# A rotation, three transformer layers and a mixture of experts on one core: layer 0 rearranged over the engines

## The chip, the cores and the metric

The kernel runs on one core of a Trainium2 chip. A core has TensorE (PE), VectorE (DVE), ScalarE (ACT), GpSimd (POOL) and SyncE (SP), which here issues the DMAs. Each works through its own list of instructions in order and waits on semaphores. Matmul results land in PSUM, eight banks of 512 fp32 columns; the other operands lie in SBUF. The metric is the device time of one execution in microseconds; three runs of the kernel before gave 2080.91 to 2091.76 us, median 2091.69.

## The reference

The input is `x` of 4 x 512 x 288 and one condition vector of 288 numbers per batch. Layer 0 comes first:

```python
U, _ = jnp.linalg.qr(P)                      # P is 288 x 64
R = expm(A)                                  # A skew, 64 x 64 per batch, its entries silu(cond) @ W.T + b
z = einsum('btn,nd->btd', x, U)
x = x + einsum('btd,nd->btn', einsum('btd,bde->bte', z, R) - z, U)
```

Three transformer layers follow. Each forms `mod = silu(c) @ w_ada + b_ada`, split in six vectors of 288 (shift, scale and gate of the attention and of the MLP), then a layernorm with shift and scale, attention with 16 heads of 18, its gated projection, a second layernorm with shift and scale, and a gated MLP of width 1152. The last layer's MLP is a mixture of four experts with the best two of each token. All is fp32.

## The kernel before

**Layer 0.** QR is done without forming the long columns. The Gram matrix of P (64 x 64) stands beside a unit matrix in `GI` (64 x 128), and the top 64 rows of P in `T`. For each of 64 columns j, PE spreads row j of `GI` over all partitions (`spread_gram`, L1416: a product with a repeated column of the unit matrix), and DVE eliminates with it (`reduce_gram`, L878 to L885). PE spreads row j of `T` as well (`spread_top`, L1423), and DVE forms sign, root and divisor and updates `T` (`reduce_top`, L895 to L910). POOL takes the square root (L733, a `pow`). `reduce_top` runs one column behind `reduce_gram`. What comes out is `RT`, which turns P into the orthonormal columns.

Between two columns PE does background work, each piece in a slot of the table `BACKGROUND` (the number is the column ahead of whose `spread_top` it stands):
- `skew`: the entries of the skew matrix, column by column, 378 instructions with up to 63 stationary columns and 4 moving ones (L1453); `turn`: its transpose (L1460). DVE adds bias and scales.
- `exp`: expm by a series of degree 6 and 14 squarings, so 19 rounds. A round is two halves of 8 products of 64 x 64 (L1476 with the matrix, L1477 with the unit matrix, which adds it); ACT copies a round's bank back (L1234).
- `x`, `y`: transposes of x (L1432) and y = P' x for each batch (L1441).
- `ada`: the modulation vectors of all three layers, three times ten pieces. The four vectors wanted along the partitions are products with 4 moving columns (L1497), the two gates products of 288 columns (L1502).

Then come the product of `RT` and expm into `Mid` (L1525, L1528), and for each batch `YM` = `Mid` y (L1535), x += `YM` PT (L1542, DVE L976). A barrier of all engines ends this phase.

**The opening.** Work is laid out in ticks: `opening()` gives the first 27 ticks (`PTICKS`), and `agenda` makes each engine's list of it. For batch 0: statistics (`stats1`, `mean1` on DVE), root and shift on POOL, normalised rows on ACT, three transposed pieces (`ln1`, L1653), five q and k pieces (`qk`) and four v pieces (`v`, both L1550), the trip of q and k through HBM into `QK` (`place`), and the first 32 score tiles (`warm`, L1572), of which DVE takes the row maxima (L996).

**Attention and MLP** follow tick by tick; the first instruction of attention proper is the first key score (L1587).

## Time and profile before

| | |
|---|---|
| runs | 2080.91 to 2091.76 us, median 2091.69 |
| the profiled execution's own time | 2106.0 us |
| its span, first to last instruction | 2104.2 us |
| PE busy, matmul | 1904.2 us (90%) |
| DVE, ACT, POOL busy | 1233.4, 924.5, 547.0 us |
| mean granted TensorE clock | 0.911 of 2.4 GHz |
| first key score (L1587) | 347.0 us |

A profile is of one execution. Busy time of PE is the time in which some matmul is in flight, and not a measure of how full the array is: an instruction of 4 moving columns counts as one of 512. PE lists each fp32 product as two instructions. The granted clock of a stretch (PEclk) reads 1.00 at 2.4 GHz and 0.50 at 1.2 GHz.

### The profile page before, as it was taken

The numbers are of one execution on the slowest core, as the hardware profiler recorded it, in microseconds if no ns is written. First come the engines' busy times: TensorE is split into PE (matmuls) and PEld (weight loads), VectorE is DVE, ScalarE is ACT, GpSimd is POOL, SyncE is SP. The second block draws the span as 40 slices with busy tenths as digits, with TensorE's granted clock in tenths as the row PEclk, the third lists the DMA queues.
The fourth block names the chain that finished last, engine by engine and source line by source line (L and its number), as shares of the span: only waits on it lengthen the run. The fifth ranks groups of instructions, "written<-read, shape, count | busy, mean of one in ns | idle before, by whom it ended". The sixth has DMA issues, their size and how long they took to land.

```text
span 2104.2 us, 29869 instructions
## 1 busy us (share of the span) xinstructions
PE 1904.2 (90%) x10842; PEld 1298.8 (62%) x10842; DVE 1233.4 (59%) x2748; ACT 924.5 (44%) x1582; POOL 547.0 (26%) x541
## 2 busy tenths in 40 slices
PE   7899858999989878999978998999989889999998
PEld 6687534444438766444435876444438778888997
DVE  6755526777735456777742655777734655546554
ACT  0200023766664434777654533767573432222221
POOL 1111131222245533333233533222141220101000
PEclk9965567999989988999987999999989999999999
DMA  7000013333210021232220021332300010001000
GB/s 236 1 1 1 8 46 93 95 101 90 93 34 10 1 80 58 86 97 79 79 73 20 4 80 50 96 106 87 104 26 35 20 31 16 26 23 34 1 23 23
DMA packets 68985, 114.08 MB, mean 54 GB/s; under 512 B 14586, under 2 KB 29498, under 8 KB 68840
## 3 DMA queue, kind: packets, MB, share of 16 engines
q1 hardware_dynamic: 68840, 112.18, 17.6%
q8 instruction: 87, 1.43, 0.3%
q14 instruction: 58, 0.48, 0.1%
HBM read 80.95 MB, written 30.70 MB: 53 GB/s over the span
## 4 chain that ended last, share of the span: by engine, by line
PE 72%; ACT 10%; DVE 9%; issue 4%; DMA 2%; POOL 2%; SPq 1%; ACTq 0%; DVEq 0%; POOLq 0%
PE ps L1550 23%; PE ps L1632 13%; PE ps L1601 8%; PE ps L1587 7%; PE ps L1678 5%; PE ps L1572 4%; ACT Pr L1373 3%; PE ps L1497 2%; PE ps L1653 2%; PE ps L1453 2%; ACT xn L1272 1%; DVE negmax L996 1%; ACT HQ L1348 1%; PE ps L1476 1%; PE ps L1477 1%
## 5 line engine op out<-in xcount | busy, mean ns | idle before, releaser
L996 DVE TENSOR_REDUCE negmax<-ps 128x1 f32<-128x512 f32 x768 | 490.1, 683 | 185.1 <-PE ps L1572 179.4
L1373 ACT ACTIVATE Pr<-ps 128x512 f32<-128x512 f32 x768 | 406.8, 601 | 155.1 <-PE ps L1587 153.6
L1384 ACT ACTIVATE g<-ps,b1col 128x512 f32<-128x512 f32 x216 | 148.5, 687 | 451.9 <-PE ps L1550 439.1
L1180 DVE CAST G<-g 128x512 fp32r<-128x512 f32 x216 | 125.9, 583 | 323.8 <-ACT g L1384 322.9
L1587 PE MATMUL ps<-QK 55*128 55x512 f32 x768 | 249.3, 515 | 53.9 <-ACT Pr L1373 51.6
L1632 PE MATMUL ps<-W2a,G 128*128 128x288 f32 x1728 | 269.7, 307 | 2.0 <-DVE G L1182 2.0
L1632 PEld LDWEIGHTS ps<-W2a,G 128*128 128x128 f32 x1728 | 251.8, 196 | 14.8 <-DVE G L1182 4.2
L1587 PEld LDWEIGHTS ps<-QK 55*128 55x128 f32 x768 | 98.4, 194 | 242.6 <-ACT Pr L1373 142.8
L1572 PE MATMUL ps<-QK 54*128 54x512 f32 x768 | 202.8, 437 | 29.2 <-DVE negmax L996 17.1
L1601 PE MATMUL ps<-Pr,V 128*32 128x512 f32 x1536 | 222.0, 652 | 0.0
L1182 DVE TENSOR_TENSOR G<-g,G 128x512 fp32r<-128x512 f32 x216 | 167.0, 773 | 7.4
L1550 PE MATMUL ps<-HQ,W1a 128*128 128x512 f32 (+1 forms) x504 | 137.4, 414 | 12.8 <-ACT g L1384 11.4
L1572 PEld LDWEIGHTS ps<-QK 54*128 54x128 f32 x768 | 95.7, 194 | 59.3 <-DVE negmax L996 38.1
L1632 PEld LDWEIGHTS ps<-W2b,G 128*128 128x128 f32 x864 | 123.1, 188 | 8.5 <-DVE G L1182 2.4
L1632 PE MATMUL ps<-W2b,G 128*128 128x288 f32 x864 | 127.1, 296 | 1.1 <-DVE G L1182 1.1
L787 POOL TENSOR_TENSOR stage<-act,stage 126x512 fp32r<-126x512 f32 (+1 forms) x60 | 77.2, 1287 | 185.7 <-ACT stage L1365 137.8
L1550 PEld LDWEIGHTS ps<-HQ,W1a 128*128 128x128 f32 (+1 forms) x504 | 94.5, 197 | 37.2 <-ACT g L1384 17.1
L1550 PEld LDWEIGHTS ps<-WQ,HQ 128*128 128x128 f32 (+1 forms) x560 | 80.5, 196 | 55.1 <-issue 22.9
L1550 PE MATMUL ps<-WQ,HQ 128*128 128x288 f32 (+1 forms) x560 | 98.6, 317 | 14.2 <-ACT HMq L1348 4.8
L1678 PE MATMUL ps<-WP,oT 128*128 128x288 f32 x384 | 110.6, 433 | 0.1
L787 POOL TENSOR_TENSOR HQ<-act,HQ 128x512 fp32r<-128x512 f32 (+1 forms) x54 | 69.6, 1289 | 140.3 <-ACT HQ L1348 139.9
L792 POOL TENSOR_TENSOR oTok<-oTok,rsum 128x512 f32<-128x512 f32 x48 | 50.3, 1049 | 208.7 <-DVE rsum L1108 207.7
(205 smaller groups left out, 2652.7 us busy)
## 6 DMA issues: line engine op xcount, KB each, us to landing
QK<-heads_t SPq DMA_DIRECT2D x192, 144.0 KB
heads_t<-stage SPq DMA_DIRECT2D x96, 252.0 KB
QK<-heads_t SPq DMA_DIRECT2D x192, 72.0 KB
raw<-in_w SPq DMA_DIRECT2D x18, 432.0 KB
raw<-in_w SPq DMA_DIRECT2D x12, 576.0 KB
WA<-in_ada_w SPq DMA_DIRECT2D x3, 1728.0 KB, 15.5
heads_t<-stage SPq DMA_DIRECT2D x24, 144.0 KB
QK<-W1a SPq DMA_DIRECT2D x192, 2.0 KB, 2.4
```

What stands on the lines that cost most here:

```text
L787: pool.tensor_tensor(lo, act32[rows, h % 2, :], hi.bitcast(F32), ALU.subtract).then_inc(low_done, 1)
L996: dve.tensor_reduce(negmax[:, m % 2, t, h:h + 1], ps[:, a_bank(s, i), :], AX, ALU.max, negate=True).then_inc(a_free, 1)
L1180: dve.tensor_copy(G[:, n % 3, 0, :], g32[:, n % 2, :]).then_inc(g_hi, 1)
L1182: dve.tensor_tensor(G[:, n % 3, 1, :], g32[:, n % 2, :], G[:, n % 3, 0, :].bitcast(F32), ALU.subtract).then_inc(g_lo, 1)
L1373: act.activation(Pr[:, t % 2, 2 * half + pair, :], ps[:, (16 * s + u) % 3, :], ACT.Exp, scale=SCALE).then_inc(b_free, 1)
L1384: act.activation(g32[:, n % 2, :], ps[:, 4, :], ACT.Gelu if l == 1 else ACT.Gelu_apprx_tanh, bias=b1col[:, e, s % FT:s % FT + 1]).then_inc ...
L1550: ins = mm(o, lhs(w, h, rows[w]), rhs(w, h, rows[w]), start=p == 0, stop=p == 6)
L1572: mm(ps[:, a_bank(s, i), :], QK[r:r + QROW, g, 0, pair, 128 * t:128 * t + 128], QK[r:r + QROW, g, 1, pair, :], start=True, stop=True).then ...
L1587: mm(ps[:, k % 3, :], QK[r:r + QROW + 1, g, 1, pair, 128 * t:128 * t + 128], QK[r:r + QROW + 1, g, 0, pair, :], start=True, stop=True).the ...
L1601: ins = mm(ps[32 * i:32 * i + 32, 6, :], V[:, s // 4 % 2, t, c:c + 32], Pr[:, t % 2, i, :], start=t == 0, stop=t == TT - 1)
L1632: ins = mm(ps[:, t, 0:C], G[:, n % 3, x, 128 * t:128 * t + 128], W2[e % 2][:, w, ft, :], start=ft == 0 and p == 0, stop=ft == FT - 1 and p ...
L1678: ins = mm(bank[:, 0:C], oT[:, (STEPS * l + 4 * i + g) % 5, 128 * k:128 * k + 128], WP[:, g, :], start=g == 0, stop=g == 3)
```

## The change

It touches layer 0, the modulation vectors and the opening:
- **Columns.** `GI` is updated in the 64 columns that are still live, `T` and its helper in those right of j. PE spreads row j twice, into one bank for DVE (65 columns) and another for ACT. ACT copies it with a factor 4 (`gram_copy`), POOL raises its diagonal entry to 0.5 and -0.5 in one instruction (`root_pair`), ACT scales the row with the second (`gram_scale`). `reduce_top` runs two columns behind.
- **Skew.** The entries of all four batches come as one row each, four times three products of 512 columns, the bias as one more row of the weights. They go to HBM and come back as 64 x 64 matrices; DVE masks them, ACT scales.
- **Expm.** A round is 8 products. The unit matrix is added ahead of it by POOL (`add_unit`, 64 x 256, two per round), and a round stands in every second column.
- **Modulation.** Each vector is a row of 4 x 288 from three products (`row_product`), bias and the 1 of the scale included in the weights. Those wanted along the partitions are turned by five small products (`turn_columns`) and copied by ACT. The six of the first transformer layer stand in the columns, the other twelve in the opening.
- **Opening.** `Mid` y and the update of x become items of the opening, batch 0 first; it has 34 ticks, and the first scores use five banks in turn. The weight splits of ACT and POOL stand in the columns (`high`, `split`), the rows of ones for `QK` are placed early.

```diff
+    for b, (t, u) in enumerate(((0, 1), (2, 3), (6, 7), (9, 10))):
+        out += [(t, "ym", 0, b, 0), (u, "l0", 0, b, 0)]
+    out += [(1, "stats1", 0, 0, t) for t in range(TT)] + [(1, "mean1", 0, 0, 0)]
+    out += [(t, "ln1", 0, 0, c) for c, t in enumerate((5, 7, 9))]
...
+    rows = [(2, 1, 0), (3, 1, 1), (4, 1, 2), (6, 1, 3), (8, 1, 4), (10, 1, 5),
+            (12, 2, 0), (16, 2, 1), (18, 2, 2), (20, 2, 3), (22, 2, 4), (24, 2, 5)]
+    for t, l, v in rows:
+        out += [(t, "arow", l, v, 0)] + ([(t + 1, "acol", l, v, 0)] if v not in (2, 5) else [])
+    out += [(t, "qk", 0, 0, j) for j, t in enumerate((11, 13, 17, 20, 23))]
...
+            def add_unit(r):
+                unit = (ident[0:D, 0:D] if r < DEGREE - 1 else ident2[:, :]).unsqueeze(1).broadcast_to([D, B, D])
+                for x in range(2):
+                    pool.wait_ge(exp_ev, 2 * r + x + 1)
+                    pool.tensor_tensor(EM[:, r % 2, x], EX[:, r % 2, x], unit, ALU.add).then_inc(exp_add, 1)
+                    pool.wait_ge(exp_add, 2 * r + x + 1)
+            def root_pair(j):
+                pool.wait_ge(g_copied, j + 1)
+                pool.tensor_tensor(roots[:, j, :], RG[:, j % 2, j:j + 1].broadcast_to([D, 2]), halves[:, :], ALU.pow).then_inc(root_ready, 1)
...
+            for j in range(D):
+                root_pair(j)
+                for slot, kind, *args in BACKGROUND:
+                    if kind == "split" and slot == j:
+                        low_weights(*args)
+                    if kind == "turn" and slot + 2 == j:
+                        add_unit(0)
+                    if kind == "exp" and slot == j and args[0] < ROUNDS - 1:
+                        add_unit(args[0] + 1)
...
             def reduce_gram(j):
-                k, r, m = j % 2, small[:, j % 2, 0:1], small[:, j % 2, 2:3]
-                row = ps[0:D, k, 0:2 * D]
+                row, m, r = ps[0:D, 0, 0:2 * D], small[:, 0:1], small[:, 5:6]
+                live = slice(j + 1, j + 1 + D)
                 dve.wait_ge(bc_g, j + 1)
                 dve.reciprocal(r, row[:, j:j + 1]).then_inc(dve_done, 1)
                 dve.wait_ge(dve_done, step())
                 dve.scalar_tensor_tensor(out=m, in0=GI[:, j:j + 1], scalar=r, in1=below[:, j:j + 1],
                                          op0=ALU.mult, op1=ALU.mult).then_inc(dve_done, 1)
                 dve.wait_ge(dve_done, step())
-                dve.scalar_tensor_tensor(out=GI[:, :], in0=row, scalar=m, in1=GI[:, :],
+                dve.wait_ge(bc_r, j + 1)
+                dve.scalar_tensor_tensor(out=GI[:, live], in0=row[:, live], scalar=m, in1=GI[:, live],
                                          op0=ALU.mult, op1=ALU.add).then_inc(gi_upd, 1)
-                dve.tensor_copy(RG[:, k, :], row[:, 0:D]).then_inc(n2_ready, 1)
             def reduce_top(j):
-                k = j % 2
-                n2, root = RG[:, k, j:j + 1], small[:, k, 1:2]
-                sg, den, rd, m, nb = small[:, k, 3:4], small[:, k, 4:5], small[:, k, 5:6], small[:, k, 6:7], NB[:, j:j + 1]
-                row = ps[0:D, 2 + k, 0:D]
-                alpha = row[:, j:j + 1]
+                row, sh = ps[0:D, 1, 0:D], SH[:, j:j + 1]
+                den, m, rd = small[:, 1:2], small[:, 2:3], small[:, 6:7]
+                alpha, live = row[:, j:j + 1], slice(j + 1, D)
                 dve.wait_ge(bc_t, j + 1)
-                dve.tensor_scalar(sg, alpha, 0.0, 2.0, ALU.is_ge, ALU.mult).then_inc(dve_done, 1)
+                dve.tensor_scalar(sh, alpha, 0.0, 0.5, ALU.is_ge, ALU.subtract).then_inc(dve_done, 1)
                 dve.wait_ge(dve_done, step())
-                dve.wait_ge(n2_root, j + 1)
-                dve.wait_ge(n2_ready, j + 1)
-                dve.tensor_scalar(nb, sg, -1.0, root, ALU.add, ALU.mult).then_inc(dve_done, 1)
-                dve.wait_ge(dve_done, step())
-                dve.tensor_scalar(den, alpha, nb, n2, ALU.mult, ALU.add).then_inc(dve_done, 1)
+                if j == D - 1:
+                    return
+                dve.wait_ge(g_scaled, j + 1)
+                dve.tensor_scalar(den, sh, roots[:, j, 0:1], alpha, ALU.mult, ALU.add).then_inc(dve_done, 1)
                 dve.wait_ge(dve_done, step())
                 dve.reciprocal(rd, den).then_inc(dve_done, 1)
+                ready = step()
+                dve.scalar_tensor_tensor(out=W[:, live], in0=RG2[:, j % 2, live], scalar=sh, in1=row[:, live],
+                                         op0=ALU.mult, op1=ALU.add).then_inc(dve_done, 1)
+                step()
+                dve.wait_ge(dve_done, ready)
+                dve.scalar_tensor_tensor(out=m, in0=T[:, j:j + 1], scalar=rd, in1=below[:, j:j + 1],
+                                         op0=ALU.mult, op1=ALU.mult).then_inc(dve_done, 1)
                 dve.wait_ge(dve_done, step())
-                dve.scalar_tensor_tensor(out=m, in0=T[:, j:j + 1], scalar=rd, in1=below[:, j:j + 1],
-                                         op0=ALU.mult, op1=ALU.mult)
-                dve.scalar_tensor_tensor(out=RG[:, k, :], in0=row, scalar=nb, in1=RG[:, k, :],
-                                         op0=ALU.mult, op1=ALU.add).then_inc(dve_done, 1)
-                dve.wait_ge(dve_done, step())
-                dve.scalar_tensor_tensor(out=T[:, :], in0=RG[:, k, :], scalar=m, in1=T[:, :],
+                dve.scalar_tensor_tensor(out=T[:, live], in0=W[:, live], scalar=m, in1=T[:, live],
                                          op0=ALU.mult, op1=ALU.add).then_inc(t_upd, 1)
...
+                act.activation(RG[:, j % 2, j:D], ps[0:D, 2 + j % 2, j:D], ACT.Copy, scale=4.0).then_inc(g_copied, 1)
...
+                act.activation(RG2[:, j % 2, j + 1:D], RG[:, j % 2, j + 1:D], ACT.Copy, scale=roots[:, j, 1:2]).then_inc(g_scaled, 1)
...
             def spread_gram(j):
                 pe.wait_ge(gi_upd, j + 1)
+                mm(ps[0:D, 0, j:j + D + 1], ident[:, j:j + 1].broadcast_to([128, D]), GIz[:, j:j + D + 1],
+                   start=True, stop=True).then_inc(bc_g, 1)
                 if j >= 2:
-                    pe.wait_ge(n2_ready, j - 1)
-                k = j % 2
-                mm(ps[0:D, k, 0:2 * D], ident[:, j:j + 1].broadcast_to([128, D]), GIz[:, :],
-                   start=True, stop=True).then_inc(bc_g, 1)
+                    pe.wait_ge(g_copied, j - 1)
+                mm(ps[0:D, 2 + j % 2, j:D], ident[:, j:j + 1].broadcast_to([128, D]), GIz[:, j:D],
+                   start=True, stop=True).then_inc(bc_r, 1)
             def spread_top(j):
                 if j > 0:
                     pe.wait_ge(t_upd, j)
-                k = j % 2
-                mm(ps[0:D, 2 + k, 0:D], ident[:, j:j + 1].broadcast_to([128, D]), Tz[:, :],
+                mm(ps[0:D, 1, j:D], ident[:, j:j + 1].broadcast_to([128, D]), Tz[:, j:D],
                    start=True, stop=True).then_inc(bc_t, 1)
...
+                for c, rows in enumerate((128, 128, 33)):
+                    ins = mm(ps[0:B, 6 + n % 2, :], csil[0:rows, c, :], Wsk[0:rows, c, N * n:N * n + N], start=c == 0, stop=c == 2)
+                ins.then_inc(skew_mm, 1)
...
+            def exp_round(r):
                 if r == 0:
...
+                for x in range(2):
+                    pe.wait_ge(exp_ev, 2 * r + 2)
+                    pe.wait_ge(exp_add, 2 * r + x + 1)
+                    for b in range(B):
+                        left = BB[:, 1 - x, b, :] if r < DEGREE - 1 else EX[:, r % 2, 1 - x, b, :]
+                        ins = mm(ps[0:D, 6 + x, D * b:D * b + D], left, EM[:, r % 2, x, b, :], start=True, stop=True)
+                    ins.then_inc(exp_mm, 1)
...
+            def row_product(l, v, bank):
+                n = AROW["arow", l, v, 0]
+                if v == 0:
                     pe.wait_ge(ada_in[l], 32)
                     pe.wait_ge(silu_done, 1)
+                if n > 0:
+                    pe.wait_ge(arow_ev, n)
+                    pe.wait_ge(acol_ev, sum(m < n for key, m in AROW.items() if key in ACOL))
+                if n == 0:
                     pe.wait_ge(y_ev, B)
...
+                for c, rows in enumerate((128, 128, 34)):
+                    ins = mm(ps[0:B, bank, 0:C], csil[0:rows, c, :], WA[l][0:rows, c, C * v:C * v + C], start=c == 0, stop=c == 2)
+                ins.then_inc(arow_mm, 1)
...
+            def turn_columns(l, v, bank):
+                n = AROW["arow", l, v, 0]
+                pe.wait_ge(arow_ev, n + 1)
+                for c in range(3):
+                    for r in range(1 if c < 2 else 3):
+                        rows = 128 if c < 2 else 32
+                        ins = mm(ps[32 * r:32 * r + rows, bank, C + B * c:C + B * c + B],
+                                 arow[:, n % 2, 128 * c:128 * c + rows], ident[0:B, 0:B], start=True, stop=True)
+                ins.then_inc(acol_mm, 1)
...
 BACKGROUND = sorted(
+    [(4 + 3 * n, "skew", n) for n in range(4)] + [(20, "turn")] + [(23 + 2 * r, "exp", r) for r in range(ROUNDS)] +
+    [(t, "x", n // 3, n % 3) for n, t in enumerate((15, 16, 17, 19, 21, 22, 26, 28, 30, 34, 36, 38))] +
+    [(t, "y", b) for b, t in enumerate((18, 24, 32, 40))] +
+    [(t, "high", n) for n, t in enumerate((28, 32, 46))] + [(t, "split", n) for n, t in enumerate((29, 33, 47))] +
+    [(50, "bias", 0)] +
+    [(t, "arow", 0, v, 5) for v, t in enumerate((42, 46, 50, 52, 56, 60))] +
+    [(t, "acol", 0, v, 5) for v, t in ((0, 44), (1, 48), (3, 54), (4, 58))], key=lambda x: x[0])
```

On DVE, one column as it repeats (before; `GI`, `T` as above, `RG` the copied row, `NB` sign and root):

```order
L878 RECIPROCAL small<-ps 64x1
L880 SCALAR_TENSOR_TENSOR small<-GI,small,below 64x1
L883 SCALAR_TENSOR_TENSOR GI<-ps,small,GI 64x128
L885 COPY RG<-ps 64x64
L895 TENSOR_SCALAR small<-ps 64x1
L899 TENSOR_SCALAR NB<-small 64x1
L901 TENSOR_SCALAR small<-ps,NB,RG 64x1
L903 RECIPROCAL small<-small 64x1
L905 SCALAR_TENSOR_TENSOR small<-T,small,below 64x1
L907 SCALAR_TENSOR_TENSOR RG<-ps,NB,RG 64x64
L910 SCALAR_TENSOR_TENSOR T<-RG,small,T 64x64
```

and now (`SH` is the sign as 0.5 or -0.5, `RG_126` the row scaled by ACT, `W` the helper):

```order
L966 RECIPROCAL small<-ps 64x1
L968 SCALAR_TENSOR_TENSOR small<-GI,small,below 64x1
L972 SCALAR_TENSOR_TENSOR GI<-ps,small,GI 64x64
L981 TENSOR_SCALAR SH<-ps 64x1
L986 TENSOR_SCALAR small<-SH,roots,ps 64x1
L988 RECIPROCAL small<-small 64x1
L990 SCALAR_TENSOR_TENSOR W<-RG_126,SH,ps 64x62
L994 SCALAR_TENSOR_TENSOR small<-T,small,below 64x1
L997 SCALAR_TENSOR_TENSOR T<-W,small,T 64x62
```

Eleven instructions become nine, and the widths shrink with the column.

On PE, a column with expm and y work before (`EF`, `BB` are the matrices of expm):

```order
L1423 MATMUL ps<-T,ident 64x64
L1416 MATMUL ps<-GI,ident 64x128
L1476 MATMUL ps<-EF,BB 64x64
L1477 MATMUL ps<-ident,BB 64x64
L1476 MATMUL ps<-EF,BB 64x64
L1477 MATMUL ps<-ident,BB 64x64
L1476 MATMUL ps<-EF,BB 64x64
L1477 MATMUL ps<-ident,BB 64x64
L1476 MATMUL ps<-EF,BB 64x64
L1477 MATMUL ps<-ident,BB 64x64
L1441 MATMUL ps<-XT,Psb 64x512 x3
L1423 MATMUL ps<-T,ident 64x64
```

and two columns with an expm round and a transpose now (`EM` is the matrix with the unit added):

```order
L1525 MATMUL ps<-GI,ident 64x65
L1530 MATMUL ps<-GI,ident 64x29
L1545 MATMUL ps<-ident,X 128x128 x4
L1536 MATMUL ps<-T,ident 64x31
L1525 MATMUL ps<-GI,ident 64x65
L1530 MATMUL ps<-GI,ident 64x28
L1583 MATMUL ps<-EM,EX 64x64 x8
L1536 MATMUL ps<-T,ident 64x30
```

One round took sixteen products, eight in a column, and takes eight in one column of two.

On PE, the end of layer 0 and the opening before (`YT`, `YM`, `PT`, `HQ_58` the layernormed x):

```order
L1535 MATMUL ps<-YT,Mid 64x512 x2
L1542 MATMUL ps<-PT,YM 128x288 x4
L1535 MATMUL ps<-YT,Mid 64x512
L1542 MATMUL ps<-PT,YM 128x288 x4
L1535 MATMUL ps<-YT,Mid 64x512
L1542 MATMUL ps<-PT,YM 128x288 x8
L1653 MATMUL ps<-ident,xn 128x128 x8
L1653 MATMUL ps<-ident,xn 96x128 x4
L1550 MATMUL ps<-HQ_58,WQ 126x512 x14
L1550 MATMUL ps<-WQ,HQ_58 128x288 x7
L1550 MATMUL ps<-HQ_58,WQ 126x512 x7
L1550 MATMUL ps<-WQ,HQ_58 128x288 x7
```

and now, with `WA_103` the modulation weights of the second layer:

```order
L1744 MATMUL ps<-YT,Mid 64x512
L1752 MATMUL ps<-PT,YM 128x288 x4
L1744 MATMUL ps<-YT,Mid 64x512
L1598 MATMUL ps<-WA_103,csil 4x288 x3
L1752 MATMUL ps<-PT,YM 128x288 x4
L1607 MATMUL ps<-ident,arow 128x4 x2
L1607 MATMUL ps<-ident,arow 32x4 x3
L1598 MATMUL ps<-WA_103,csil 4x288 x3
L1607 MATMUL ps<-ident,arow 128x4 x2
L1607 MATMUL ps<-ident,arow 32x4 x3
L1598 MATMUL ps<-WA_103,csil 4x288 x3
L1769 MATMUL ps<-ident,xn 128x128 x4
```

The four updates of x stood together; now the first stands alone, and row products and turned columns stand between the others and the layernorm.

## Rows read from the trace of the kernel before

**Rows 1.** Windows, all engines: start:end, length, busy us (x instructions), PEclk, DMA share, GB/s.

```profile
62.00:120.00 58.00, 50.26 (x418) 35.40 (x418) 42.83 (x218) 13.52 (x23) 10.84 (x20) 0.94 0.01 2
120.00:256.00 136.00, 124.07 (x856) 103.68 (x854) 74.38 (x363) 6.50 (x11) 20.24 (x32) 0.57 0.01 2
256.00:281.00 25.00, 15.80 (x50) 8.13 (x50) 10.64 (x28) 7.43 (x13) 7.01 (x8) 0.77 0.03 8
281.00:347.00 66.00, 43.77 (x124) 25.43 (x124) 21.48 (x38) 17.18 (x29) 15.67 (x15) 0.58 0.30 92
347.00:2104.20 1757.20, 1622.24 (x8951) 1085.79 (x8950) 1046.61 (x1933) 875.91 (x1502) 484.07 (x440) 0.95 0.18 54
```

**Rows 2.** Chain that ended last, 8 to 256 us, share by line.

```profile
by line: PE ps L1497 18.6%; PE ps L1453 12.9%; PE ps L1476 9.0%; PE ps L1477 8.9%; PE ps L1416 8.2%; PE ps L1423 6.6%; PE ps L1502 6.0%; PE ps L1441 4.4%; issue 3.4%; DVE small L901 2.5%; DVE GI L883 2.2%; DVE T L910 2.1%; DVE small L905 2.
```

**Rows 3.** Instruction groups of PE, 8 to 256 us: busy us, mean ns.

```profile
L1497 PE MATMUL ps<-csil,WA 128*32 128x4 f32 (+1 forms) x360 | 52.3, 257 | 4.8 <-DVE grow L948 4.8
```

**Rows 4.** Timeline of DVE, one column: start us, duration us, instruction.

```profile
97.40 0.28 DVE L910 SCALAR_TENSOR_TENSOR T<-RG,small,T 64x64 f32<-64x64 f32 x1
97.60 0.15 DVE L878 RECIPROCAL small<-ps 64x1 f32<-64x1 f32 x1
97.79 0.21 DVE L880 SCALAR_TENSOR_TENSOR small<-GI,small,below 64x1 f32<-64x1 f32 x1
98.04 0.34 DVE L883 SCALAR_TENSOR_TENSOR GI<-ps,small,GI 64x128 f32<-64x128 f32 x1
...
98.44 0.14 DVE L895 TENSOR_SCALAR small<-ps 64x1 f32<-64x1 f32 x1
98.61 0.21 DVE L899 TENSOR_SCALAR NB<-small 64x1 f32<-64x1 f32 x1
98.86 0.27 DVE L901 TENSOR_SCALAR small<-ps,NB,RG 64x1 f32<-64x1 f32 x1
99.16 0.15 DVE L903 RECIPROCAL small<-small 64x1 f32<-64x1 f32 x1
99.35 0.21 DVE L905 SCALAR_TENSOR_TENSOR small<-T,small,below 64x1 f32<-64x1 f32 x1
99.49 0.27 DVE L907 SCALAR_TENSOR_TENSOR RG<-ps,NB,RG 64x64 f32<-64x64 f32 x1
99.79 0.28 DVE L910 SCALAR_TENSOR_TENSOR T<-RG,small,T 64x64 f32<-64x64 f32 x1
```

**Rows 5.** Timeline of PE and DVE, the two hand-offs of a column.

```profile
95.67 0.33 PE L1423 MATMUL ps<-T,ident 128*64 128x64 f32 x2
...
96.04 0.15 DVE L895 TENSOR_SCALAR small<-ps 64x1 f32<-64x1 f32 x1 [1.91 <-PE ps L1423]
...
97.73 0.33 PE L1423 MATMUL ps<-T,ident 128*64 128x64 f32 x2 [0.92 <-DVE T L910]
...
98.43 0.69 PE L1416 MATMUL ps<-GI,ident 128*64 128x128 f32 x2 [0.38 <-DVE GI L883]
```

**Rows 6.** Timeline of PE, three products of 512 and of 288 columns.

```profile
92.86 2.88 PE L1441 MATMUL ps<-XT,Psb 128*64 128x512 f32 x6
...
200.42 3.13 PE L1502 MATMUL ps<-WA,csil 128*4 128x288 f32 x6
```

**Rows 7.** Timeline of POOL and DVE, 247 to 252 us.

```profile
247.98 4.08 POOL L738 TENSOR_TENSOR WQ<-raw,WQ 128x864 fp32r<-128x864 f32 x2
...
250.22 1.92 DVE L910 SCALAR_TENSOR_TENSOR T<-RG,small,T 64x64 f32<-64x64 f32 x1
```

**Rows 8.** Timeline of POOL and DVE, 1640 to 1643 us.

```profile
1640.76 1.45 POOL L751 TENSOR_TENSOR rstd<-var,neghalf 128x4 f32<-128x4 f32 x1
...
1641.69 0.69 DVE L1182 TENSOR_TENSOR G<-g,G 128x512 fp32r<-128x512 f32 x1
```

**Rows 9.** Timeline of PE, first `ln1` product and first key scores.

```profile
281.17 1.09 PE L1653 MATMUL ps<-ident,xn 128*128 128x128 f32 x4 [8.43 <-ACT xn L1275]
...
347.00 1.21 PE L1587 MATMUL ps<-QK 55*128 55x512 f32 x2
```

563 lines of the change are left out of this document (293 added, 270 removed).

## The prediction

> **What bounds the kernel now.** I read the windows first, cut where the work changes. The QR and expm phase ends at 256 us, the opening (the layer 0 update, the first layernorm, q, k, v of batch 0 and the first scores) takes from there to 347 us, and the remaining 1757.2 us run at a granted clock of 0.95 [rows 1, 9]. The change leaves the instructions behind 347 us in their order, so I look for its whole effect ahead of that point. In the chain of waits of 8 to 256 us nearly every named share is PE's [rows 2]: the modulation products (L1497) 18.6%, the skew products (L1453) 12.9%, the expm products (L1476 and L1477) 17.9%, against 6.8% of the three DVE lines that it still lists in full or in part. In the last 136 us of it PE is busy 124 at a granted clock of 0.57 [rows 1], so most of that work ran at the lower level, 1.2 GHz.
>
> The second view is the timeline of one column that no background work of PE holds up. DVE needs 2.39 us for it (97.40 to 99.79, from one T to the next) [rows 4]. 64 columns of that are 153 us, while 248 pass between 8 and 256. The other 95 us are PE work that stands between two columns and is not covered. Both parts are touched by the change.
>
> **The column.** From 11 DVE instructions it goes to 9: the copy of the row goes to ACT, the scaling by the root to ACT and POOL, and GI is updated in 64 columns, not 128. I put it together from start-to-start distances of rows 4: reciprocal to m 0.19, m to GI 0.25, GI (64 wide, like T to reciprocal) 0.20, sign to den 0.17, den to its reciprocal 0.30, that to W 0.14 (as L905 to L907, no wait between), W to m 0.20, m to T 0.25, T to the next reciprocal 0.20. That is 1.90, and about 1.85 as W and T grow narrower. PE has to keep up in that time. T to the start of its product takes 0.33 and from there to the sign 0.37 [rows 4, 5], 0.70 in all, while DVE has 0.84 of other work in between, so it doesn't wait. Sum: column 0 starts near 5.8 us (an estimate: two memsets stand ahead of it on DVE instead of eight, two loads fewer are waited for), first two columns 2.7, 62 columns of 1.85 are 115, the end 2: 125.5 us.
>
> **PE work between the columns.** After GI PE starts 0.39 later [rows 4, 5], spreads two rows of 65 and on average 32 columns, and is wanted again by T one column on. By these distances 0.9 us are free at the higher clock and 0.7 at the lower: background beyond some 0.8 us per column shows. Prices: three products of 512 columns take 2.9 us at 2.4 GHz, three of 288 take 3.1 at 1.2 GHz [rows 6]. So three of 512 are 2.6 to 5.1 without the tail, three of 288 are 1.5 to 3.0, eight of 64 are 0.9 to 1.8.
> - Skew, 378 tiny matmul instructions now, becomes 4 rows of three 512-column products. I take 3.5 each, 2.7 uncovered: 11 us.
> - Four y products of the same size: 11 us. Twelve transposes nearly fit: 2 us.
> - Expm: 19 rounds of 8 products instead of 16, one round every second column. I take 1.3 each, 0.5 uncovered: 9 us.
> - Row products of the first transformer layer, six at 2.2: 8 us; their four turned columns: 2 us. The turn of the skew matrix, where PE waits for DVE and DVE for PE: 2 us. Its trip through HBM lies between columns 13 and 20, over 12 us, and costs nothing; without that cover it would be some microseconds, once.
> - POOL. It now adds the unit, 64x256 twice a round. One 128x864 subtraction takes 2.04 [rows 7], so 256 columns are about 0.6. Beside those two subtractions L910, which reads two tiles in SBUF, took 1.92 us instead of 0.28 [rows 4, 7] and ended with the second of them. Three DVE instructions of a new column have two such inputs (both m and T). 38 additions of 0.6, hitting at any phase, delay by 0.2 each on average where DVE isn't waiting anyhow: 7 us. The three weight splits that move from behind the columns into them delay by most of their 2.04: 5 us.
>
> Uncovered: 57 us. Bounds: all at 2.4 GHz and POOL's additions in DVE's own waits, 22; all at 1.2 GHz and each addition fully waited for, 106. The columns then end at 182.5 us (147 to 231), where they end at 256 now: 73 us earlier. ACT and POOL have 2.4 columns, over 4 us, for the hand-over of a row (copy, root, scale), which I cost at nothing.
>
> **The rule that speaks against it.** The Trainium skill, page "SBUF — State Buffer", section "SBUF: two separate sides", says of the port pair that VectorE and GpSimd share that the one that starts first has it for its whole instruction and the other is blocked entirely. The T of rows 7 agrees with it. The root (`pow`) does not: while L751 ran from 1640.76 to 1642.21, an L1182 with two inputs in SBUF started at 1641.69 and took its usual 0.69 [rows 8]. So I count the 64 roots at nothing. What the root would cost if it did hold the port is a rival below.
>
> **The opening.** It takes 91 us now, with PE busy 15.8 of 25 and 43.8 of 66 us, so 31 idle, at clocks of 0.77 and 0.58 [rows 1]. Into it come 12 row products (1.5 to 3.0) and 8 turned columns. For one of these I take 10 matmul instructions at the 257 ns of L1497 [rows 3], which overlap by half, hence 0.8 to 1.6. Together that is 24 to 49 us of PE work, in a stretch that becomes denser, so nearer to the lower end: 34. They stand between the pieces of the q, k, v chain, whose waits are PE's idle time; I let 22 be filled. The update of batch 0 ahead of the others lets the statistics start some 9 us sooner, but PE has to pass the other three updates before the first q product in any case; I count 4. 91 + 34 - 22 - 4 = 99 us. Bounds: 87 (all of it in idle time) to 140 (nothing is hidden, low clock).
>
> **Sum.** First scores of attention at 182.5 + 99 = 281.5 instead of 347: 65.5 us less. The profiled execution took 2106.0 us, so 2040.5 by its own measure. It lies 14 us above the median of 2091.69 shown, so the forecast for a median is 2026 us, 3.1% faster.
>
> **Rivals.**
> - *High clock and full cover.* PE's dense streams of 288 and 512 columns keep the clock up, and the row products vanish in idle time. Columns end at 155, opening 91: 246, so 101 us less, 1991. For: in 62 to 120 us the clock read 0.94 with such streams [rows 1]. Against: between the streams the new columns ask still less of PE. Chance 0.17.
> - *The root holds the port*, or the hand-over over ACT and POOL comes late. By the distances of rows 4 and 5 the root starts about 1.4 us after GI and ends 0.6 or 0.7 later, and the m of the next GI stands at 1.58: it would wait 0.5 in each of 62 columns, 31 us: 2057. This is what the skill's rule makes of it; rows 8 speak against. Chance 0.15.
> - *Slower: the opening becomes a chain on one bank.* All 12 row products and 8 columns go through PSUM bank 4, each waits for ACT's copy of the last, and whatever stands behind on PE waits with it. At 1.2 GHz that is 49 us of work and 20 hand-overs; at 1.5 us each with no idle time used, 79 more: 170. With the columns at 213 (the rival above) that is 383, 36 us later than now: 2128. It decides once columns and opening together exceed 347. Against it: 31 us of idle PE, and other banks for everything else. Chance 0.03.
> - *The shorter rounds don't shorten anything*, because each waits for ACT and POOL, and no more than 0.5% is gained. A ring of PE, two copies and two additions of 0.6 needs about 4 us, two columns 3.7. Chance 0.02.
>
> **Numbers.** Forecast 0.63, its own range 2010 to 2044. With the rivals the range is 1993 to 2062. A change under 0.5% (10 us) could not be told from none. Faster 0.95, same 0.02, slower 0.03.
>
> **What would show it.** Right: the last column near 180 us, columns without background near 1.85 us, first key scores near 280, the rest within 1757 us and a few. POOL's additions beside a stretched m or T, and none beside a root. Wrong: every column over 2.3 us with a stretched m (the port), PE idle in columns while DVE waits for the scaled row (the hand-over), an opening well over 110 us with PE waiting for ACT's copies of rows (the bank), or a change behind the first scores, which no step here allows for.

## The result: 1.0% faster where 3.1% was forecast

The changed kernel takes 2069.6 us in the median of 5 runs (2061.37 to 2071.78), the kernel before 2087.11 beside it (2080.91 to 2091.76): ratio 0.9903, 95% interval 0.9875 to 0.9932. The same kernel, run once more for the experiments, gives 2064.93 and 0.9893 (0.9872 to 0.9915). The direction is right. The gain is some 20 us, a third of the 65.5 that I summed up, and the time lies above the range of 1993 to 2062.

Windows of the changed kernel, cut where its work changes (columns as in [rows 1]):

```profile
62.00:120.00 58.00, 49.38 (x304) 33.90 (x302) 39.08 (x182) 22.20 (x74) 30.79 (x40) 0.59 0.03 7
120.00:195.00 75.00, 67.38 (x408) 44.78 (x409) 44.00 (x234) 21.41 (x90) 34.01 (x47) 0.52 0.00 1
195.00:318.00 123.00, 98.21 (x325) 45.27 (x326) 31.87 (x66) 28.12 (x66) 19.36 (x21) 0.62 0.14 42
318.00:2059.60 1741.60, 1599.77 (x8951) 1072.07 (x8949) 1046.69 (x1933) 878.63 (x1504) 485.35 (x441) 0.96 0.18 55
```

The QR and expm phase ends at 195 us instead of 256, 61 earlier. The opening takes 123 us instead of 91, and gives 32 of them back. The granted clock is 0.59, 0.52 and 0.62 in the three stretches: in 62 to 120 us, where [rows 1] had 0.94, it is low as well.

A column that no background work holds up, by DVE's timeline of the changed kernel. It answers to [rows 4], and POOL's root beside it is the last row:

```profile
114.42 0.24 DVE L997 SCALAR_TENSOR_TENSOR T<-W,small,T 64x29 f32<-64x29 f32 x1
114.59 0.15 DVE L966 RECIPROCAL small<-ps 64x1 f32<-64x1 f32 x1
114.78 0.21 DVE L968 SCALAR_TENSOR_TENSOR small<-GI,small,below 64x1 f32<-64x1 f32 x1
115.02 0.28 DVE L972 SCALAR_TENSOR_TENSOR GI<-ps,small,GI 64x64 f32<-64x64 f32 x1
115.29 0.15 DVE L981 TENSOR_SCALAR SH<-ps 64x1 f32<-64x1 f32 x1
...
116.24 0.24 DVE L997 SCALAR_TENSOR_TENSOR T<-W,small,T 64x28 f32<-64x28 f32 x1
```
```profile
114.44 0.70 POOL L815 TENSOR_TENSOR roots<-RG,halves 64x2 f32<-64x2 f32 x1
```

T to T is 1.82 us (forecast 1.85). The root ran from 114.44 to 115.14, and a T and an m (L968) with two inputs in SBUF took their usual 0.24 and 0.21 beside it: no wait for the port. Beside a weight split it is otherwise:

```profile
93.63 2.05 DVE L997 SCALAR_TENSOR_TENSOR T<-W,small,T 64x35 f32<-64x35 f32 x1
```
```profile
93.63 2.00 POOL L822 TENSOR_TENSOR WQ<-raw,WQ 128x864 fp32r<-128x864 f32 x1
```

What one piece of background costs PE, from the chain of waits (start, duration): two skew rows, a y product, an expm round.

```profile
13.99 4.61 PE ps L1565 x6
...
23.31 5.30 PE ps L1565 x6
...
58.09 4.76 PE ps L1554 x6
...
73.19 1.90 PE ps L1583 x16
```

[Rows 6] has 2.88 for three products of 512 columns at the higher level; these are nearer to the lower one, as the granted clock of 0.59 and 0.52 says. I had taken 3.5, 3.5 and 1.3.

The opening, first on PE and then on ACT. L1598 is a row product, L1769 a turn of xn, L1637 a q or v product, L1663 the query scores:

```profile
215.52 3.13 PE L1598 MATMUL ps<-WA,csil 128*4 128x288 f32 x6 [0.44 <-ACT ada L1340]
219.14 1.22 PE L1607 MATMUL ps<-ident,arow 4*128 4x4 f32 x10 [0.49 <-ACT arow L1333]
220.79 3.13 PE L1598 MATMUL ps<-WA,csil 128*4 128x288 f32 x6 [0.44 <-ACT ada L1340]
226.94 1.12 PE L1769 MATMUL ps<-ident,xn 128*128 128x128 f32 x4 [3.02 <-ACT xn L1376]
...
261.65 1.20 PE L1637 MATMUL ps<-WQ,HQ 128*128 128x288 f32 x7 [1.24 <-ACT stage L1478]
275.23 1.22 PE L1663 MATMUL ps<-QK 54*128 54x512 f32 x4 [12.38 <-DMA QK<-heads_t]
```
```profile
223.96 0.40 ACT L1333 ACTIVATE arow<-ps 4x288 f32<-4x288 f32 x1 [3.31 <-PE ps L1598]
224.27 2.17 ACT L1373 ACTIVATE xn<-X,shift,rstd 128x288 f32<-128x288 f32 x4
```

PE has 12.38 us of idle time in one piece, waiting for the DMA of the heads, and no row product stands there. Seven stand ahead of it and five behind it, and ACT scales xn only after the third row copy.

### The profile page after: what moved, and what is told of

Read it like the earlier page. It is cut to its first block, busy times and chain, and to the rows that moved or that the text cites. A ratio compares the mean times of both kernels' runs of the same rounds, so it can differ in the third digit from the quotient of the medians.

```text
span 2059.6 us, 28854 instructions
## 1 busy us (share of the span) xinstructions
PE 1862.0 (90%) x10144; PEld 1215.4 (59%) x10144; DVE 1192.9 (58%) x2584; ACT 964.4 (47%) x1778; POOL 584.9 (28%) x585
## 4 chain that ended last, share of the span: by engine, by line
PE 72%; ACT 10%; DVE 9%; issue 4%; DMA 2%; POOL 1%; SPq 1%; ACTq 0%; DVEq 0%; POOLq 0%
PE ps L1637 23%; PE ps L1726 13%; PE ps L1695 8%; PE ps L1681 7%; PE ps L1794 5%; PE ps L1663 4%; ACT Pr L1486 3%; PE ps L1598 2%; PE ps L1769 2%; ACT xn L1373 2%; PE ps L1583 1%; DVE negmax L1050 1%; DVE X L1068 1%; ACT HQ L1461 1%; DMA heads_t<-stage 1%
## 5 line engine op out<-in xcount | busy, mean ns | idle before, releaser
L1726 PE MATMUL ps<-W2a,G 128*128 128x288 f32 x1728 | 263.8, 303 | 7.2 <-DVE G L1241 5.7
L1726 PEld LDWEIGHTS ps<-W2a,G 128*128 128x128 f32 x1728 | 245.8, 192 | 20.5 <-DVE G L1241 10.4
L1663 PE MATMUL ps<-QK 54*128 54x512 f32 x768 | 198.9, 433 | 33.4 <-DVE negmax L1050 14.9
L1695 PE MATMUL ps<-Pr,V 128*32 128x512 f32 x1536 | 217.2, 639 | 0.0
L1637 PE MATMUL ps<-HQ,W1a 128*128 128x512 f32 (+1 forms) x504 | 134.5, 407 | 12.8 <-ACT g L1497 11.4
L1663 PEld LDWEIGHTS ps<-QK 54*128 54x128 f32 x768 | 93.1, 192 | 61.1 <-DVE negmax L1050 34.3
L1637 PEld LDWEIGHTS ps<-HQ,W1a 128*128 128x128 f32 (+1 forms) x504 | 93.2, 194 | 36.0 <-ACT g L1497 16.4
L1637 PEld LDWEIGHTS ps<-WQ,HQ 128*128 128x128 f32 (+1 forms) x560 | 79.4, 193 | 51.9 <-issue 24.2
L1637 PE MATMUL ps<-WQ,HQ 128*128 128x288 f32 (+1 forms) x560 | 97.1, 314 | 12.5 <-ACT HMq L1461 4.8
```

The costliest lines, as they stand in the source:

```text
L1637: ins = mm(o, lhs(w, h, rows[w]), rhs(w, h, rows[w]), start=p == 0, stop=p == 6)
L1663: mm(ps[:, row_bank(l, s, i), :], QK[r:r + QROW, g, 0, pair, 128 * t:128 * t + 128], QK[r:r + QROW, g, 1, pair, :], start=True, stop=True) ...
L1695: ins = mm(ps[32 * i:32 * i + 32, 6, :], V[:, s // 4 % 2, t, c:c + 32], Pr[:, t % 2, i, :], start=t == 0, stop=t == TT - 1)
L1726: ins = mm(ps[:, t, 0:C], G[:, n % 3, x, 128 * t:128 * t + 128], W2[e % 2][:, w, ft, :], start=ft == 0 and p == 0, stop=ft == FT - 1 and p ...
```

## Experiments

Each kernel was timed against the kernel before in five rounds on the same chip; ratios are to that. "Columns end" is the first product with RT (194.8 in the changed kernel's first profile), "opening" the time from there to the first key scores.

**1. The changed kernel again.** No edit.

> The changed kernel as it is, once more. In the two profiles so far the first key scores come at 318.1 us instead of 347.0 (28.9 earlier), and what lies behind them is 15.7 us shorter, 44.7 in all, while the medians differ by 17.5. Theory A: the stretch behind the first scores varies from execution to execution, and the true gain is about 20 us: the ratio to the kernel before comes out at 0.990, the first key scores of a new profile at 318 within 2 us, and the rest behind them at more than 1745. Rival B: the later layers really are shorter: ratio near 0.980, the rest again at 1741.5.

2064.93 us, ratio 0.9893. Columns end at 193.6, first key scores at 320.4, the rest is 1746.2. Theory A holds, though the first scores lie just outside its 318 within 2 us.

**2. The kernel before again.** No edit.

> The kernel before, once more, for a profile that is not 19 us above its median. Its first key scores come at 347.0 in the first profile, the changed kernel's at 318.1 and 320.4, so 27 to 29 are won ahead of them, but the medians differ by 20 to 22. Theory A (part of it is given back behind the first scores): in this profile the first scores come again at 347 and what lies behind them takes 1740 or less, against 1741.5 and 1746.2 in the changed kernel. Rival B (the rest is alike and the profile of before was only an outlier in its opening): first scores at 340, rest 1745.

Ratio 0.9984 (0.9961 to 1.0008). Its windows:

```profile
62.00:120.00 58.00, 50.35 (x410) 35.23 (x411) 42.44 (x216) 13.55 (x23) 10.87 (x20) 0.94 0.01 2
120.00:247.00 127.00, 114.51 (x865) 95.64 (x863) 74.78 (x365) 6.50 (x11) 20.28 (x32) 0.63 0.01 3
247.00:338.00 91.00, 59.63 (x174) 33.60 (x175) 32.12 (x66) 24.58 (x41) 22.70 (x23) 0.63 0.23 69
338.00:2088.00 1750.00, 1610.83 (x8951) 1077.51 (x8950) 1045.93 (x1933) 875.32 (x1502) 484.50 (x440) 0.96 0.18 54
```

Here the columns end at 247, not 256 [rows 1], at a clock of 0.63 instead of 0.57 behind 120 us. The first scores come at 337.8. Rival B is nearer: the first profile of before was 9.2 us late ahead of the first scores and 7 behind them (1757.2 against 1750). Nothing is given back behind the first scores: 1750 and 1746 in these two executions. Taken from this pair, the change wins 17.5 us ahead of them and 4 behind.

**3. Wide rows.**

```
-ps[0:B, 6 + n % 2, :], csil[0:rows, c, :]   # csil [128, 3, 4]
+ps[:, 6 + n % 2, :], csil[0:rows, c, :]     # csil [128, 3, 128], the 4 columns 32 times
```

> The skew rows and all 18 row products are made with csil repeated 32 times, so that they fill 128 rows of PSUM instead of 4; number of instructions and streamed columns are the same. Theory 1 (PE's clock is the mis-sized term): before the change the clock stayed at 1.00 until 80 us with wide products, after it fell to 0.53 at 20 us when the skew rows (4 rows of output) began. With wide ones the clock in 20 to 60 us is 0.9 or more, a skew row takes 2.7 us instead of 5.3, a row product 1.6 to 2.3 instead of 3.1; columns end 8 to 15 us earlier than 194.8, and the first key scores come 15 to 30 us earlier than 318.1: ratio to before 0.975 to 0.985. Rival 2 (the number of waits and small pieces between the columns sets the clock): granted clock and the 4.8 and 3.1 us stay as they are, time the same as the changed kernel within 3 us.

2068.56 us, ratio 0.9915 (0.9895 to 0.9935). Columns end at 193.3, first scores at 321.2. The four skew rows took 4.23, 4.86, 5.23 and 5.79 us. The clock of 20 to 60 us reads 0.66, but the columns end where they did: those with a y product are 2.4 us shorter in all than in experiment 1, those with a row product 2.5 longer, since a wide row product takes 3.55 us where the narrow one takes 3.13. The time is rival 2's.

**4. Wide rows and wide expm products.** As 3, with EX, EM and BB on 128 partitions (64 of zeros) and `left` two blocks wide where it can be.

> As the kernel with the wide rows, and the expm products get 128 contracted rows (64 of them zeros, as they had before the change) and mostly 128 rows of output instead of 64 by 64. Theory 1: an expm round falls from 1.93 to 1.1 us, so that the clock in 80 to 190 us rises from 0.5 to 0.6 up to 0.8 or more, columns end at 175 us or before, first key scores below 295, ratio to before 0.96 to 0.975. Rival 2: the rounds stay at 1.9 us and the time at that of the kernel with wide rows alone.

2101.86 us, ratio 1.0078 (1.0053 to 1.0102): slower than the kernel before. Columns end at 227.9. PE's timeline of it, a skew row and an expm round, and the window around the skew row:

```profile
36.36 5.79 PE L1572 MATMUL ps<-Wsk,csil 128*128 128x512 f32 x6
...
118.34 3.85 PE L1593 MATMUL ps<-EM,EX 128*128 128x64 f32 x16
```
```profile
36.00:42.00 6.00, 6.00 (x10) 1.94 (x9) 1.36 (x8) 0.00 (x0) 0.00 (x0) 1.00 0.21 69
```

The eight products with 128 rows and (mostly) 128 outputs take 3.85 us instead of 1.97 at the same clock, and 2.17 at the higher one. The granted clock rose little for it: 0.67 instead of 0.59 from 60 to 120 us, and 0.53 in both from 120 to 180. So the round of 64 by 64 is cheap at 1.2 GHz already, and widening it doubles its price for almost no clock. Theory 1 was half wrong: the price at the lower clock is the mis-sized term, but not one that these edits give back. The window shows why I had misread it. It says 1.00 while three products of 512 columns take 5.79 us, more than a y product takes in the stretches of 0.5 to 0.6 (4.76). The trace's clock records begin at 51.4 us here and at 17.8 us in the changed kernel; ahead of the first record a window reads 1.00 whatever the speed. The "fall at 20 us" on which this expectation rests was the first record.

**5. Rows in attention.** All 12 row products and 8 turned columns leave the opening and go through bank 7 into the attention of layer 0.

```
-for t, l, v in rows: out += [(t, "arow", l, v, 0)] ...      # opening, bank 4
+if l == 0 and b < 2: ... out += [(t, "arow", b + 1, v, 0)]  # attention window, bank 7
```

> The 12 row products and 8 turned columns of the second and third transformer layer leave the opening and go through bank 7 into the attention of layer 0, batches 0 and 1. Theory 3 (they stand in order in the opening, with ACT's scaling of xn behind them): the opening falls from 123.4 us to 95 or less (12 times 3.1 and 8 times 1.2 are 47 us of PE work, and 15 us in which xn waited for ACT), first key scores at 290 or earlier; attention of layer 0, with PE busy 95%, takes 12 times 1.6 and 8 times 0.6, some 24 us, more than its 275, so that the time is within 10 us of the changed kernel. Rival 4 (the opening is bound by its own chain of q, k, v and the DMA of the heads, the row products only fill its waits): opening 115 us or more, and the time 15 to 25 us worse than the changed kernel's.

2049.4 us, ratio 0.9824 (0.9802 to 0.9847), 0.7% better than the changed kernel. Opening 91.0 us instead of 126.8 in experiment 1; attention of layer 0 291.1 instead of 272.6. Theory 3 holds for the opening and the attention; the time is 15.5 us below the changed kernel's, where it had said within 10. First query and first key scores on PE:

```profile
248.74 1.22 PE L1676 MATMUL ps<-QK 54*128 54x512 f32 x4 [12.15 <-DMA QK<-heads_t]
...
283.86 0.63 PE L1694 MATMUL ps<-QK 55*128 55x512 f32 x2
```

From the end of the columns to the first query scores it is 55.9 us, with the rows 83.8: 27.9 more. Seven row products and five turned columns stood there: 7 x 3.13 and 5 x 1.2 are 27.9 (27.4 by their durations in experiment 1). They cost their work one for one, and the wait of 12 us stayed beside it.

**6. Rows in the gap.** As 5, but rows 0, 1 and 2 of the second layer stand in the opening behind the first v product.

> As the kernel with the rows in attention, but three of the row products and two of the turned columns come back into the opening, behind the first v product, where PE waits 12.15 us for the DMA of the heads. Theory 3 (it is the place in PE's order that costs, not the work): at 1.2 GHz they are 3 times 3.1 and 2 times 1.2 with five hand-overs of 0.5, 14 us, of which 12 are covered; first key scores at 284 to 287, attention of layer 0 some 6 us shorter, time 3 to 5 us better than the kernel with all rows in attention. Rival 4 (opening bound elsewhere, pieces of PE there cost in full): first key scores at 298, time 6 us or more worse.

2061.06 us, ratio 0.9859 (0.9826 to 0.9892). First query scores at 263.7, 14.5 us after those of 5 by their distance from the columns' end: the rival's number, but not its reason. SP's queue shows it:

```profile
232.66 1.61 SPq L692 DMA_DIRECT2D heads_t<-stage  x2
251.36 0.26 SPq L680 DMA_DIRECT2D gate_rows<-arow  x1
251.66 1.52 SPq L692 DMA_DIRECT2D heads_t<-stage  x2
257.16 0.32 SPq L709 DMA_DIRECT2D QK<-heads_t  x1
```

The DMA of the gate row waits on SP for the third row copy, and the second store of heads, ready near 237, waits behind it until 251.66.

**7. The splits behind the columns, too.** As 6, with `(28, 32, 46)` and `(29, 33, 47)` of BACKGROUND taken out and "split" items at ticks 3, 3 and 6 of the opening. ACT's halves of the splits, the bias and one load move with POOL's.

> As the kernel with rows in the gap, and POOL's three weight splits go out of the columns into the opening. Theory 5 (a split holds up the m or T of the column beside it: 93.63 2.05 T, 108.25 1.94 den, 148.81 2.06 T): the columns end 5 to 6 us earlier and the time is 4 to 6 us better. Rival 6 (PE is the bound in those columns too, so a late T is covered by its background): columns end within 1.5 us of before, time the same within 2 us, or worse, because the splits now hold up the layer 0 update.

2051.29 us, ratio 0.981 (0.9777 to 0.9843). Columns end at 185.2 instead of 193.3: 8.2 us. Theory 5, somewhat more than priced. Of the 8.2, 5.7 lie in the three columns in which a split had held a T or an m (the 29th, 33rd and 47th distance from T to T: 11.12 us together, now 5.47). The rest is spread over others, some of them ahead of the first split (the 17th is 1.5 shorter), and doesn't come back in experiment 10, whose columns have the same program and end at 188.7.

**8. Sixteen products.**

```
-mm(o, left, EM..., start=True, stop=True)
+mm(o, left, EX..., start=True, stop=False); mm(o, left, one, start=False, stop=True)   # POOL's add_unit empty
```

> The changed kernel, with the unit added by eight more products in each expm round, as before the change, and without POOL's 38 additions. Theory 1 (the products are PE-bound at 1.2 GHz, 1.97 us for eight): a round takes 3.9 us, the columns end 25 to 37 us later, the time is 25 to 37 us worse than the changed kernel: so the shorter rounds are worth about 1.5 us each, more than the 0.5 to 1.3 by which I priced them. Rival 7 (POOL's additions cost what the shorter rounds save): time within 10 us of the changed kernel.

2081.35 us, ratio 0.9961 (0.9935 to 0.9988). Columns end at 213.6, 20 us later; the time is 0.7% worse. Between theory and rival. Against experiment 13, which has eight products and no additions either, the columns end 25 us later: that is what the shorter rounds are worth. What POOL's additions take back follows there.

**9. Rows in attention and splits behind the columns.** 5 with the edit of 7.

> All 12 row products in the attention of layer 0, as in the fourth experiment, and the three splits behind the columns, as in the seventh. If both gains are their own (columns 8.2 us earlier at 185.2, opening some 36 us shorter), the first key scores come at 276, and the time is 22 to 25 us below the changed kernel: 2040 to 2045, ratio to before 0.977 to 0.979. If the splits in the opening hold up the layer 0 update once the rows are gone, the first scores stay near 280 and the time near 2047.

2042.26 us against 2082.42, ratio 0.9807 (0.9779 to 0.9835). Columns end at 185.3, first scores at 276.5. In the profile both gains are there in full, the columns 7.5 us earlier than in 5 and the opening at 91.2. This is the lowest ratio of the study, 1.9% under the kernel before, but its interval overlaps those of 5, 7 and 10. Its opening, the attention of layer 0 and the rest:

```profile
185.00:276.50 91.50, 64.29 (x173) 34.98 (x175) 31.81 (x68) 25.22 (x42) 25.43 (x24) 0.59 0.19 59
276.50:567.50 291.00, 274.33 (x1534) 122.62 (x1530) 182.84 (x323) 192.12 (x372) 76.25 (x70) 0.96 0.28 83
567.50:2036.00 1468.50, 1349.33 (x7569) 959.28 (x7569) 864.34 (x1610) 691.89 (x1161) 408.71 (x371) 0.96 0.16 49
```

The rows' work is now in a stretch at a clock of 0.96, where PE is busy 94% and some 18.5 us pay for all 20 pieces (291.0 against 272.65 in experiment 1).

**10. The gap without a gate row.** As 9, with rows 0, 1 and 3 of the second layer (each with its turned column) behind the first v product.

> As the last one, with rows 0, 1 and 3 of the second transformer layer back in the opening, behind the first v product. In the sixth experiment that place cost 14.6 us, and the trace shows why: the DMA of the gate row (row 2) stood on SP ahead of the second store of heads and waited for ACT's row copy at 250.9, so the heads were stored at 251.7 instead of at 237. Theory 3a (the queue, not PE's order, made it dear): without a gate row among them the first query scores move by 3 to 5 us only and the time is within 2 us of the kernel with all rows in attention. Rival (PE in order): first query scores 10 us or more later, time 5 us or more worse.

2044.93 us, ratio 0.9815 (0.9789 to 0.9842). From columns' end to the first query scores 55.5 us, against 56.0 in 9 with nothing there. PE:

```profile
239.43 3.13 PE L1613 MATMUL ps<-WA,csil 128*4 128x288 f32 x6 [0.34 <-ACT ada L1353]
243.05 1.22 PE L1625 MATMUL ps<-ident,arow 4*128 4x4 f32 x10 [0.49 <-ACT arow L1343]
244.19 1.22 PE L1678 MATMUL ps<-QK 54*128 54x512 f32 x4
```

Three products and three turned columns are hidden whole, and the wait for the heads is gone. Theory 3a is shown for the place; what it is worth in time is not. The attention is 4 us shorter (481.9 to 485.8 us from first key scores to those of the next layer), but this execution's columns ended 3.3 later than 9's, and the times can't be told apart.

**11. Rows behind xn.** The opening's first seven rows at ticks 8, 9, 10, 10, 11, 12 and 14 instead of 2, 3, 4, 6, 8, 10 and 12.

> The changed kernel with all 12 row products in the opening, but the first ones stand behind the first layernorm's products in the tick table (ticks 8 to 14 instead of 2 to 12). The statistics of batch 0 are ready at 209.5, yet ACT scales xn only at 224.3, since three row copies stand ahead of it. If the 15 us are lost to ACT's order, q starts earlier but the rows are still in front of the heads' wait: first scores 5 to 15 us earlier than 319, time 5 to 15 us better. If PE's row products cost their own length wherever they stand ahead of the heads (12 times 3.1 and 8 times 1.2), nothing changes: first scores 316 to 322, time the same within 3 us.

2054.36 us, ratio 0.9864 (0.9829 to 0.9899), against 0.9893. Opening 117.0 us, 9.8 shorter; xn's first turn on PE starts at 210.4 instead of 225.7 in experiment 1. ACT's order was worth 10 us, not the 15 by which xn was late. Only 5.0 of them lie ahead of the first query scores (78.8 against 83.8): there seven row products and five turned columns, 25.5 us, still cost 23.0 over experiment 5, nearly their whole work.

**12. Batch 0 not first.** ym and l0 at ticks (0, 1), (2, 3), (3, 3), (4, 4).

> The changed kernel with the updates of batches 2 and 3 moved ahead of the first layernorm, so that all four are done first, as before the change. I priced batch 0 first at 4 us. If so, the time is 2 to 6 us worse. If xn waits for row copies anyway (224.3), the order of the updates is worth nothing: first scores and time the same within 2 us.

2067.92 us, ratio 0.9922 (0.9895 to 0.995). Opening 126.6 us against 126.8. In this kernel batch 0 first is worth nothing that shows.

**13. No additions.**

> The changed kernel with POOL's 38 additions of the unit left out (the expm is then computed without the added unit). I priced them at 7 us, through delays of DVE's m and T on the shared port. In the changed kernel a column with a round takes 2.75 us on average against 1.80 for one with nothing, and eight products take 1.97 of PE. If the additions cost what I said, those 19 columns take 2.4 and the columns end at 186 to 187 instead of 193 to 195, the time is 5 to 8 us better. Rival (PE's eight products at 1.2 GHz are all of the excess, the additions hide): columns end and time within 2 us of the changed kernel.

2061.59 us, ratio 0.9873 (0.9844 to 0.9902). Columns end at 188.2, 5.4 us earlier; the time can't be told from the changed kernel's. The number is near my theory's, but not for its reason: the columns with a round hardly moved (2.74 to 2.77 on average, not 2.4). 5.3 of the 5.4 us lie in the three columns in which a split had held a T or an m (11.12 us together, now 5.80); the other 59 take 170.1 and 170.0. Without the additions POOL comes to each split some microseconds sooner, one column earlier, beside an expm round of PE. One m in a held column of experiment 1, and then a split of this kernel:

```profile
107.00 2.00 POOL L822 TENSOR_TENSOR WQ<-raw,WQ 128x864 fp32r<-128x864 f32 x1
```
```profile
107.08 1.93 DVE L968 SCALAR_TENSOR_TENSOR small<-GI,small,below 64x1 f32<-64x1 f32 x1
```
```profile
102.01 2.01 POOL L818 TENSOR_TENSOR WQ<-raw,WQ 128x864 fp32r<-128x864 f32 x1
```
```profile
102.31 1.72 DVE L990 SCALAR_TENSOR_TENSOR small<-T,small,below 64x1 f32<-64x1 f32 x1
```

Two m are still held for 1.5 us each in this kernel, but their columns grew by 1.3 and 0.6 only. That leaves some 2 us for the 38 additions, an estimate from these columns. DVE's timeline of experiment 1 agrees: beside additions six T and m took longer than usual, by 2.5 us in all, and the longest was

```profile
106.18 0.79 DVE L997 SCALAR_TENSOR_TENSOR T<-W,small,T 64x31 f32<-64x31 f32 x1
```

No run has neither splits nor additions in the columns.

**14. Rows of one third.**

```
+if l > 0 and c < 2: continue    # in row_product: the third matmul alone
```

> The changed kernel, where each of the 12 row products in the opening is its third matmul alone (34 rows, the one with the bias; the two of 128 rows are left out), with all copies, turned columns and waits in place. Taking the rows out whole made the opening 36 us shorter (from 127 to 91), for 47 us of PE work. If it is PE's work in a full row that costs (the clock at 1.2 GHz), 2.1 us go in each of 12: 25 us less if all stand in line, first scores at 294 to 300. If hand-overs between PE and ACT on the one bank cost (0.45 to 0.5 each, and the wait of xn behind row copies), the opening keeps 25 or more of the 36 us, and the first scores come at 305 or later.

2053.59 us, ratio 0.985 (0.9818 to 0.9882). First scores at 311.1. Up to the first query scores it is 71.4 us, 12.4 less than 83.8, for 7 x 2.0 of work taken out: again nearly one for one. Behind them it is 46.1 instead of 43.0, since the clock stayed low there (a row product of experiment 1 took 1.7 us from 289 on). There a turned column took 1.22 us, against 0.77 in experiment 1. The numbers are my second theory's (305 or later, 25 or more kept), but the hand-overs are not the cause, since up to the first query scores the work taken out came back nearly one for one. Neither theory had it as it is: the work costs in full where it stands ahead of the heads, and only seven of twelve stand there.

## Why the prediction was wrong

Against the pair of experiments 1 and 2, the first scores came 17.5 us earlier, where I forecast 65.5. The 48 us between are three terms.

**The opening, 28 us.** The step "they stand between the pieces of the q, k, v chain, whose waits are PE's idle time; I let 22 be filled" failed. I put 34 us of work into 31 us of idle time by its sum, and did not ask where in PE's order the idle time lies. In the kernel before, its longest pieces were 8.43 us for xn and 5.41 for the heads. In the changed order without the rows (experiment 5) one wait for the DMA of the heads is 12.15, and seven of the products stand ahead of the q and k products that start this DMA, not in the wait. They and five turned columns cost 27.9 us, their whole work, with no filling at all. The other five and three turned columns cost 8 of 13. Net 36 where I had 12: by durations in experiment 1 the 20 pieces are 40 us of work, not 34, and 4 of them were filled, not 22. The price was low too: 3.13 us for the rows ahead of the heads, where I took some 2, nearer to the lower end because a "denser" stretch would be faster. It was not, at a clock of 0.62. The gain of batch 0 (4 us) is not there: experiment 12 shows none beside the rows, and without rows the opening is 91.0, as before. With the rows in it, xn stood behind row copies on ACT (experiment 11). The rival of the chain on one bank named the right place, but the hand-overs on it are 0.44 to 0.49, not 1.5, and work in order was the cost.

**The columns, 11 us.** From one T to the next in experiment 1, by what stands on PE between them (start times of L997; what is above 1.80 us is uncovered):

| background | columns | mean, us | uncovered, us | forecast, us |
|---|---|---|---|---|
| none | 12 | 1.77 | 0 | 0 |
| skew row | 4 | 6.02 | 16.9 | 11 |
| y product | 4 | 5.32 | 14.1 | 11 |
| expm round | 19 | 2.74 | 17.9 | 9 |
| row product | 6 | 3.77 | 11.8 | 8 |
| turned column | 4 | 2.29 | 2.0 | 2 |
| transposes | 12 | 2.33 | 6.4 | 2 |
| skew turn | 1 | 2.66 | 0.9 | 2 |
| POOL | | | in the above | 12 |

70 uncovered instead of 57. POOL's part is smaller than I had it: 5.7 for the splits (experiment 7; forecast 5) and some 2 for the additions (experiment 13; forecast 7, though an addition takes 0.72 us and not 0.6). That leaves about 62 for PE, where I had 45. So PE's prices were short by some 17 us, and the term for the additions, about 5 too high, hid part of it by luck. I had priced each product between its costs at the two levels of the clock, and most of them ran at or near the lower, as the 0.57 of [rows 1] said for the last 136 us of the kernel before. Sixteen of the nineteen expm rounds of experiment 1 took 1.97 us, and three 1.14. The 0.94 of 62 to 120 us had pulled me up. The base (first T at 10.5, 62 columns of 1.8, the end 1.9: 124) was 125.5.

**The measure, 9 us.** I set the gain against first scores at 347.0. A second profile of the same kernel has them at 337.8. The 14 us by which I lowered the total for the median were partly this, so a gain measured from 347 was counted too high.

**Right.** The column (1.82), and the root, beside which two-input instructions took no longer, while a split held T for 2.05 us. Of the rule in the Trainium skill ("SBUF — State Buffer", section "SBUF: two separate sides"), that the engine which starts first has the shared port pair for its whole instruction, the trace agrees for the split and disagrees for the root; with it the 62 columns would have been 0.5 us longer each, by the prediction's estimate. The hand-over of a row was never late. Behind the first scores no difference shows: in nine profiles of kernels that are alike there, the changed one among them, the rest takes 1736.2 to 1753.7 us, and 1757.2 and 1750.4 in the two of the kernel before. A difference of some microseconds there can't be read from one profile of each.

## What to carry to other kernels

Idle time can't be filled by its sum: for each piece that is added, name the wait that it stands directly in front of in its engine's order, and count it in full if there is none. Then follow its DMA as well: one gate row on SP's queue turned a free place into one of 14.5 us. And take the price of PE work from the clock of the stretch into which it goes, not from the middle of the two levels. When a run with one term taken out gives the forecast number, look at which columns gave it: without the additions, the splits had moved.

## What the runs showed that I had not expected

- Products of 64 by 64 take 1.97 us per eight at 1.2 GHz, eight on 128 rows and mostly 128 outputs 3.85; in the stretches of the higher clock it is 1.14 and 2.17.
- A window's clock reads 1.00 ahead of the trace's first clock record (15.9 to 68.4 us in these profiles), while a row of three 512-column products took 4.6 (13.99 us of the changed kernel) and 5.8 us there (experiment 4). The durations tell the speed.
- Profiles of one kernel differ by 9 us ahead of the same product, with a granted clock of 0.57 and 0.63 from 120 us to the columns' end.
- A GpSimd addition of 64x256 took 0.72 us, and 38 of them between DVE's short instructions held these up by 2.5 us in all.
